# Causal attention: the eight value projections stand among the first group's scores instead of in front of them

## What is computed

```
h = layernorm(layernorm(x)) * g + b
q, k, v = split16(h @ Wq + bq), split16(h @ Wk + bk), split16(h @ Wv + bv)   # 16 heads of 16 channels
att = softmax(where(causal, q @ k.T / 4, -inf))                               # 1024 x 1024 for each head
x = x + concat(att @ v) @ Wp + bp
```

## Time and profile before

| | |
|---|---|
| median of 3 runs | 4305.14 us (4296.96 to 4316.94) |
| profiled execution, its own time | 4313.47 us |
| its span, first to last instruction | 4311.7 us |
| PE, DVE, ACT busy | 82%, 53%, 35% of the span |
| mean granted TensorE clock | 0.915 of full speed |

### The profile page before, as it was taken

The page is one execution under the profiler, slowest core; times in us unless marked ns, Lnnn a source line. Parts: engine busy times, 40 slices in busy tenths (PEclk is TensorE's granted clock), DMA queues, the critical chain, the costliest instruction groups (busy, mean ns, idle before and its releaser), DMA issues.

```text
span 4311.7 us, 55263 instructions
## 1 busy us (share of the span) xinstructions
PE 3544.3 (82%) x21566; PEld 1905.3 (44%) x21566; DVE 2280.4 (53%) x5155; ACT 1523.4 (35%) x2282; POOL 353.6 (8%) x270
## 2 busy tenths in 40 slices
PE   5388878878878849999779798797987988888889
PEld 2233333343343338888435334453344543444534
DVE  8865466466466436666463443724446344364343
ACT  3134424334333423443342323433225332244322
POOL 6000001000100124444000000000000000000000
PEclk8688988988988869999999899899999999999989
DMA  3221231131040168777210302102120122101130
GB/s 120 84 69 16 71 94 16 53 111 16 20 145 9 27 152 221 225 224 206 55 35 21 56 12 51 35 1 39 49 51 16 21 33 55 45 16 26 26 62 11
DMA packets 206360, 279.59 MB, mean 65 GB/s; under 512 B 100816, under 2 KB 164962, under 8 KB 190116
## 3 DMA queue, kind: packets, MB, share of 16 engines
q1 hardware_dynamic: 189065, 255.41, 22.5%
q0 software_dynamic: 17024, 20.53, 2.4%
HBM read 199.30 MB, written 75.14 MB: 64 GB/s over the span
## 4 chain that ended last, share of the span: by engine, by line
PE 52%; DVE 25%; DMA 8%; ACT 7%; issue 4%; SPq 2%; POOL 1%; DVEq 0%; ACTq 0%; another core or an unknown queue 0%
PE ps L860 6%; PE ps L1365 5%; DVE max_parts L2018 4%; PE ps L807 4%; PE ps L809 4%; PE ps L808 4%; PE ps L996 3%; PE ps L956 3%; PE ps L1211 3%; PE ps L1218 3%; DMA x_tokens<-scr_x_normalised,arena 2%; PE ps L979 2%; DVE minus_max_context L2154 2%; ACT arena L1535 2%; PE ps L1139 2%
## 5 line engine op out<-in xcount | busy, mean ns | idle before, releaser
L860 PE MATMUL ps<-ternary_W,ident 128*128 128x512 f16 x2420 | 741.3, 417 | 123.7 <-ACT arena L1596 36.8
L2018 DVE TENSOR_REDUCE max_parts<-ps 128x1 f32<-128x512 f32 (+3 forms) x768 | 387.2, 552 | 210.4 <-PE ps L959 161.0
L1467 ACT ACTIVATE arena<-ps 128x256 f32<-128x256 f32 (+7 forms) x512 | 319.1, 650 | 465.1 <-PE ps L979 288.3
L860 PEld LDWEIGHTS ps<-ternary_W,ident 128*128 128x128 f16 x2420 | 239.3, 104 | 466.5 <-issue 144.1
L956 PE MATMUL ps<-k_stack,q_stack 96*128 96x512 f16 (+3 forms) x768 | 265.5, 381 | 76.6 <-DVE max_parts L2018 33.9
L1535 ACT ACTIVATE arena<-ps 77x1024 f32<-77x1024 f32 x192 | 190.4, 1016 | 273.8 <-PE ps L1131 268.8
L1938 DVE CAST arena<-arena 128x256 f16<-128x256 f32 (+3 forms) x424 | 160.8, 379 | 235.2 <-ACT arena L1633 151.1
L2432 DVE TENSOR_REDUCE max_parts<-ps 128x1 f32<-128x512 f32 x256 | 170.6, 689 | 171.9 <-PE ps L1338 169.3
L979 PE MATMUL ps<-q_stack,k_stack 98*128 98x512 f16 (+3 forms) x768 | 236.1, 353 | 30.4 <-ACT arena L1467 27.1
L1940 DVE TENSOR_TENSOR arena<-arena 128x256 f16<-128x256 f32 (+3 forms) x424 | 246.1, 580 | 14.6
L1697 ACT ACTIVATE arena<-ps 128x1024 f32<-128x1024 f32 x128 | 130.5, 1023 | 337.1 <-PE ps L1354 337.1
(11 more groups left out here) (433 smaller groups left out, 7259.4 us busy)
## 6 DMA issues: line engine op xcount, KB each, us to landing
arena<-scr_expert_weights SPq DMA_DIRECT2D x52, 1024.0 KB, 7.4
k_stack<-scr_expert_weights SPq DMA_DIRECT2D x26, 1024.0 KB, 7.6
q_stack<-in_exp_W SPq DMA_DIRECT2D x16, 1024.0 KB, 10.6
scr_expert_weights<-k_stack SPq DMA_DIRECT2D x16, 1024.0 KB, 4.9
q_stack<-scr_q SPq DMA_DIRECT2D x120, 128.0 KB, 3.9
scr_q<-arena SPq DMA_DIRECT2D x48, 256.0 KB, 2.9
k_stack<-scr_q SPq DMA_DIRECT2D x72, 128.0 KB, 4.1
scr_q<-arena SPq DMA_DIRECT2D x16, 512.0 KB, 4.2
```

The source lines that it names most:

```text
L860: pe.matmul(s[:, 0:CH], ident[:], Wq1[:, 0, 0:CH], start=True, stop=True)
L1467: act.activation(PR[:, n % NP, kt * P:T], slot(L, "ST", g, kt, j)[:, kt * P:T], ACT.Exp).then_inc(*did("act", L, "exp", g, kt, j))
L2018: dve.tensor_reduce(mpart[:, j * NT + t, c:c + 1], slot(L, "S", g, t, j, c)[:, 0:n], AX, ALU.max).then_inc(*frees("dve", L, "S", g, t, j, c))
```

## The change

The eight value projections become steps `("V", t)` of the list, each behind the four score steps of its query tile, for group 0 alone. On PE the loop over the tiles becomes a function that these steps call, and the bank comes from the ring of four. ACT's program is not changed: it still copies all eight value banks before its first exponential. DVE and SP pass over the new steps.

```diff
-    steps = [("S", 0, t, j) for t in range(NT) for j in range(GH)] + [("MT", 0)]
+    steps = [step for t in range(NT) for step in [("S", 0, t, j) for j in range(GH)] + [("V", t)]] + [("MT", 0)]
...
-                for t in range(NT):
-                    s = claim("S", L, "v", t)
+                def values(t):
+                    s = claim("SB", L, "v", t)
                     for k in range(KD):
                         split3(s[:, 0:D], parts(XT, k, slice(t * P, (t + 1) * P)),
                                (Wf[:, wi[L + "v"], 0, k, :], Wf[:, wi[L + "v"], 1, k, :]), k == 0, False)
                     bias_rows(s[:, 0:D], L + "v", P).then_inc(*did("pe", L, "v", t))
+
                 steps = own_attention_steps(led.batch > 0)
...
-                    g = step[1] if len(step) > 1 else None
+                    g = step[1] if len(step) > 1 and kind != "V" else None
+                    if kind == "V":
+                        values(step[1])
```

## The result

The changed kernel takes 4325.2 us (median of 20 runs, 4312.0 to 4342.2), the kernel before 4313.2 us (20 runs alternating with them on the same chip, 4297.0 to 4321.9). The ratio is 1.0034 with a 95% interval of 1.0022 to 1.0045. On 4313.2 us that is 14.7 us slower (9.5 to 19.4); the two medians themselves lie 12.0 us apart, inside this interval. The forecast was 14.0 us, 0.33%, and 4325.2 us lies in its range of 4300 to 4338. So it is a small loss, and the interval leaves no doubt about its sign: 20 executions of each kernel resolve much less than the 0.5% that the prediction took for the least that can be told. On a second chip the ratio was 1.0037 (1.0025 to 1.0048).

A forecast was written before the change was run, and what follows sets the result against it. The k spill and its way back bound the kernel up to the first score, then DVE's 48 maxima, not PE. +16.4 - 0.8 - 1.1 - 0.5 = +14.0 us gave 4319 us, 0.33% slower, range 4300 to 4338.

The forecast's parts named there:

- The wait in front and what leaving it gives: Before the first score: values leave PE's wait for the k stack, whose DMA comes no earlier; 0.8 us won.
- Holes on DVE: In the 48 maxima: DVE waits for PE behind value tiles; 4.1 us a batch, 16.4 us for four.
- the formula: DVE's gap behind each value tile: 0.15 us + values + next tile's first score - three queued maxima.
- The clock: After PE's idle wait, scores begin at 1.2 GHz and stay there for 2.9 to 6.8 us; 5 taken.
- What is given back: Behind the maxima: PE at 2.4 GHz turns them sooner, 1.1 us, and first turned score comes sooner, 0.5 us.
- the turn: PE's turn of the maxima after DVE's reduction no longer stands behind slow fillers: 0.37 x 3 = 1.1 us won.
- The clock stays low: Rival: short bank waits hold 1.2 GHz over the whole score stretch; 41 us of loss in all, 4345 us; chance 0.08.
- falls again: Rival: the clock rises but falls at tiles 4 to 6; 17 us on top, 4336 us; chance 0.10.
- The clock comes back at once: Rival: at once or never low, only gaps at 2.4 GHz stay; +6 us, 4311 us; chance 0.12.
- All is hidden: Rival: PE gets far enough ahead, DVE keeps its 22.4 us; 2.4 us given back, 4303 us; chance 0.10.
- The values of tile 7: End of the score stretch: done with the fillers at 1.88 us, before the reduction's end at some 2.1; hidden.
- ACT's table load: Its 1.28 us move behind the last values but are covered before the first exponential; otherwise 1.3 us a batch.

The follow-up runs named there:

- the fillers' kernel: The changed kernel with 40 filler matmuls of 512 columns in PE's wait for the k stack: stretch of maxima 24.48 us, 1.0035 of the kernel before.
- the A ring: The changed kernel with the values claiming banks A0 and A1 instead of the scores' ring of four, no fillers: 1.0028 of the kernel before.
- three tiles in front and the A ring: The changed kernel with values on banks A0 and A1, tiles 0 to 2 made in the wait; without fillers 1.0001 of the kernel before.
- 28 fillers in the wait: The changed kernel with values on A0 and A1, tiles 0 to 2 made in the wait and 28 filler matmuls behind them: 1.0056 of before.
- with 22: The changed kernel with values on A0 and A1, tiles 0 to 2 made in the wait and 22 filler matmuls behind them: 1.0024 of before.

## Why the prediction was right

**The wait in front and what leaving it gives.** The values cost next to nothing where they stood, and the DMA did not come earlier without them. In the third and fourth batch of the kernel before, the k stack had landed 0.64 and 0.40 us ahead of the first score, against 0.05 in the other two, so the copy of the last values cost 0.9 us together (0.5 in the profile of the second chip); the term was -0.8. The whole wait moved by -1.4 in the first pair of profiles and 0.0 in the second. It holds the stack's landing too, which moves by 0.7 us either way in each batch.

**Holes on DVE.** Forecast +16.4 us with the later first maximum in it; measured 16.8 + 0.4 = 17.2 (first pair) and 15.0 + 0.4 = 15.4 (second pair). Tile by tile at 2.4 GHz the fillers' kernel gives the formula within 0.03 us. In the change the holes behind tiles 0, 1, 2, 4, 5 are 1.82, 1.75 to 1.41, 0.11, 0.45 and 0.18 us against 1.81, 1.53, 0.13, 0.46, 0.20; on the second chip that of tile 1 is 0.72 to 1.41. One reason in it was off: behind tile 0 it is PE's own pace at 1.2 GHz, and not the release of a bank, as the A ring showed. The right figure there was luck. The first maximum comes 0.1 us later behind the first score in each batch, as forecast.

**The clock.** Forecast low for 2.9 to 6.8 us with 5 taken; measured 6.1, 5.3, 5.7, 5.3 us, and 3.9 to 5.3 on the second chip. Each us of it moves the stretch by 0.48 us, as long as it ends at tile 1; that is the scatter of the stretch from 25.8 to 26.8.

**What is given back.** Forecast -1.1 for the turn and -0.5 for the first turned score. The turn measured -1.1 in both pairs, the rest -1.3 in the first pair and 0.0 in the second: there the rows of before gave only a bound.

**The sum.** Between the marks it is 16.8 + 0.4 - 2.4 = 14.8, the 14.9 taken directly (15.0 + 0.4 - 1.1 = 14.3 on the second chip). It lies inside the interval of the whole time, 9.5 to 19.4. That forecast and measurement lie as close as 14.0 and 14.7 is in part luck: in the first pair the holes cost 0.8 us more than forecast and 0.8 more was given back.

**The rivals.** *The clock stays low* and *falls again* are refuted: it is 1.00 from 293 to 314 us, through tiles 4 to 6 and up to the last values, and likewise in the other batches. The Trainium skill (TensorE: Matmul & The Clock Gate, section on a second failure mode by cycling through PSUM banks) says that short idle times between groups of matmuls, while banks are cycled, make the gate swing. The trace of the change does not agree: banks are cycled and PE waits for them, 3.1 of 21 us, and the granted clock stays at 1.00. With less work between the scores it did fall: in the kernel before at 295.2, and with a quarter of the values' work for 3.4 to 6.8 us in the middle or at the end of the stretch in each batch. So *falls again* was a real possibility, and the two traces suggest, without showing it, that the full work of the values kept it away. *The clock comes back at once* is refuted by 4 to 6 us at 0.50; its stretch is that of the fillers' kernel, 24.48. *All is hidden* is refuted by the holes; only with three tiles in front and the A ring was DVE kept busy with values among the scores. The values of tile 7 were hidden, and ACT's table load was too: its next exponential came 4 us behind it.

## What to carry to other kernels

Work of an idle engine can be free in a wait for a DMA and cost time beside the engine that sets the pace, although the idle engine has room there on average. Between two scores only the work that the slower engine has queued (here three maxima, 0.6 to 1.8 us) covers it. Emptying the wait also left the next stretch with a low clock here. So ask what work will stand first behind the wait: scores alone kept DVE busy even at 1.2 GHz, scores with values among them did not. Where such work has to move, put it behind the tiles whose queued work is longer than it, and on banks of its own.

## What the hardware showed that I had not expected

- On the second chip PE stops for over 6 us in the middle of batches 2 and 3 with no releaser shown (6.39 us above), in the unchanged program; the whole kernel takes some 28 us longer there (4341.4 against 4313.2 us).
- With 28 fillers in the wait a second stop of about 5 us appeared at the head of the passes of a loop 1.3 ms and more later, and was gone with 22 and with 40.
- Filling the whole wait kept the clock up and shortened the stretch as computed, and still cost 0.2 to 0.3% elsewhere. That was measured in four kernels on two chips; neither its cause nor its exact place was found, and the wait moved by the same edit is not ruled out.
